# Gate choice, bias spreading and experts in one program, in all four mixture layers of an eight-layer graph model

## The chip, the cores and the metric

One core of one Trainium2 chip runs the whole model in one launch. The metric is the device time of the launch in microseconds, the median of three runs. The compute engines are TensorE (PE; its weight loads are shown as PEld), VectorE (DVE), ScalarE (ACT) and GpSimd (POOL); SyncE (SP) issues DMAs. They run their own instruction streams and meet through semaphores. All numbers here are float32.

## The reference

x is [32, 256, 128]: 8192 tokens of 128 features. Eight layers follow one another, each added to x after a row normalisation. Four of them are mixtures of experts, and only these change:

```python
x = x + _L0_ffn_ref(_layernorm(x), ...)   # 8 experts, gelu, weights = 2 largest of softmax(logits)
x = x + _L1_ffn_ref(_layernorm(x), ...)   # 4 experts, gelu, scores from a graph attention, softmax over top 2
x = x + _L2_ffn_ref(_layernorm(x), ...)   # 6 experts of three products, relu, softmax of the softmax's top 2
x = x + _L3_ffn_ref(_layernorm(x), ...)   # 8 experts, relu, softmax over top 2
# each of them, for a token: sum over experts e of  gate[e] * (act(x @ W1[e] + b1[e]) @ W2[e] + b2[e])
```

gate[e] is zero for all but two experts. The kernel splits the last bias off: it adds the sum of gate[e] * b2[e] with one small product for all experts.

## The kernel before

**Tiles.** x stays on chip as `top_x`, 64 tiles of 128 tokens. The transposed, normalised x of a layer (`xnT`) is also on chip. Four tiles make a group of 512 columns; there are NG = 16 groups.

**Stages.** Each layer is a row of stages, each an `nc.Block` with one program for each engine; a stage starts when all engines have ended the one before. In the mixture layers, written l0f, l1f, l2f and l3f in the names of tiles, the last two are the gates stage (`gates`, L379) and the experts stage (`slotted_experts`, L559, in l0f and l3f; `experts`, L476, in l1f; `experts3`, L977, in l2f).

**The gates stage.** PE makes one product (L403) with every expert's bias for every lane, and ACT spreads it into `biases` with 16 activations (L424). DVE meanwhile picks the two largest scores (`top2`, L360 to L367), hands one tile to ACT for an exponential (L428 or L430; in l2f there is a second one, L433), and works out the gates; its last instruction (L469) writes `top_gate`. PE then turns the gates (L407), ACT copies them (L435, `gT`), and PE and DVE go through the 16 groups: a product `gT` times `biases` (L415) into one of two PSUM buffers `pb`, and the add to x (L472). PE may run two groups ahead of DVE.

**The experts stage.** For each group and expert there is a step. Its up part is two products of 512 columns into `pu` (L495 in l1f, L627 in l0f and l3f); ACT turns each into `h` (L523, L768) with gelu or relu; its down part is eight products of 128 columns into `py` (L503, L635); DVE adds `py` times the gate to x with four instructions (L536, L855). PE issues the up part of the next expert before the down part of this one. A down part waits for its own two `h` tiles and for DVE's add of two steps before; an up part waits until ACT has freed one of four `pu` buffers; `h` waits for the down part of two steps before. In l2f a step is one product (L998), ACT, one product (L1004), ACT, and four products of 128 columns (L1011), three steps deep. Groups are hardware loops (`Fori`) on PE and ACT, and written out on DVE.

**The slots of l0f and l3f.** Only half of the tiles go through all experts. The tokens of the other 32 tiles are sorted by expert into slots: two ranking products on PE (L620, L621) into `tp`, a chain on DVE (L798 to L815) that ends with `slots_ready`, 64 indirect DMAs by POOL that scatter the rows (L714, one pair for each add of DVE), and a slot stage after the first FIRST = 4 groups, that is after 32 steps. In l0f DVE also does counting work for a later layer beside the steps (`fill`, up to 1.7 us a step; L1630, L1636), and in both `owners()` hands out small pieces of work one by one.

Of the kernel before, what the change touches and what calls it, by code (L numbers as in the profile page):

```python
# [7 lines left out]
P = 128  # L8
# [4 lines left out]
GRP = 4  # L13
# [365 lines left out]
def gates(nc, g, tag, E, kind, b2, logits=None, score_bias=None, scores=None, choice=None):  # L379

    with Scope(nc, tag) as s:
        s.rev8 = g.rev8
        lg = s.sb("lg", [P, T, E])
        sel1, sel2, w1, w2 = choices(s, E) if choice is None else choice
        tmp = s.sb("tmp", [P, T, E])
        m1 = s.sb("m1", [P, T])
        m2 = s.sb("m2", [P, T])
        rr = s.sb("rr", [P, T])  # L390
        e2 = s.sb("e2", [P, T])
        su = s.sb("su", [P, T])
        gT = s.sb("gT", [P, T // BLOCK, P])
        biases = s.sb("biases", [P, BLOCK, D])
        pr = s.ps("pr", [P, COLS])
        pw = s.ps("pw", [P, COLS])
        pb = s.ps("pb", [P, 2, COLS])
        (dve_step, exp_in, exp_out, gate_ready, spread_mm, spread_done, gt_mm, gt_copied, bias_mm, bias_added) = s.sems(
            "dve_step", "exp_in", "exp_out", "gate_ready", "spread_mm", "spread_done", "gt_mm", "gt_copied", "bias_mm", "bias_added")
        with nc.Block() as block:  # L400
            @block.tensor
            def _(pe):
                nc.tensor.matmul(pw[:, 0:D], g.expert_lanes[0:E, :, :].rearrange("e t k -> e (t k)"), b2,  # L403
                                 start=True, stop=True).then_inc(spread_mm, 1)
                pe.wait_ge(gate_ready, 1)
                for q in range(T // BLOCK):
                    last = nc.tensor.transpose(pr[:, bass.ts(q, P)], g.gate[:, bass.ts(q, BLOCK), :].rearrange("p t e -> p (t e)"),  # L407
                                               g.ident[:, :])
                last.then_inc(gt_mm, 1)
                pe.wait_ge(spread_done, BLOCK)  # L410
                pe.wait_ge(gt_copied, 1)
                for m in range(NG):
                    if m >= 2:
                        pe.wait_ge(bias_added, m - 1)
# [61 lines left out]
def experts(nc, g, tag, xnT, E, W1, b1, W2, CH, func):  # L476

    with Scope(nc, tag) as s:
# [5 lines left out]
        with nc.Block() as block:  # L485
            @block.tensor
            def _(pe):
# [3791 lines left out]
```

## Time and profile before

| | us |
|---|---|
| runs | 5020.86, 5023.57, 5030.29 |
| median | 5023.57 |
| profiled execution | 5024.53 |
| its span in the trace | 5022.8 |

Busy shares over the span: PE 69%, DVE 67%, ACT 34%, POOL 20%. The model is a row of stages with different limits, so these shares say little on a change within four of them; the views of those stages say more.
### The profile page before, as it was taken

How to read it: one execution, taken by the hardware profiler on the slowest of the kernel's cores; microseconds unless marked ns; L12 is line 12 of the kernel's file. 1: busy time of each engine (PE TensorE's matmuls, PEld its weight loads, DVE VectorE, ACT ScalarE, POOL GpSimd, SP SyncE). 2: the span in 40 equal slices, each digit the busy share in tenths (PEclk: the TensorE clock that was granted, in tenths of full speed). 3: DMA queues.
4: the chain of work that ended last, by engine and by line, in shares of the span. 5: the costliest groups of instructions: out<-in, count | busy, mean ns of one | idle time of the engine just before them, and what ended most of it. 6: DMA issues, size and time to landing. Idle time of an engine off the chain costs nothing. (4 is left out here: it accounts for less than half of the span.)

```text
span 5022.8 us, 67345 instructions
## 1 busy us (share of the span) xinstructions
PE 3450.1 (69%) x17032; PEld 2647.6 (53%) x17034; DVE 3350.8 (67%) x17506; ACT 1694.9 (34%) x4351; POOL 1009.0 (20%) x1111
## 2 busy tenths in 40 slices
PE   7888854552330022779966588889899789786997
PEld 6888844551110021557744477757745346575675
DVE  7998998779998998477756566643334544425444
ACT  2222233334342221034435122244365345432343
POOL 0000000325542001024410477600001000000414
PEclk9999999999755555989978555589999899887999
DMA  3000000000000000112211311000000000000022
GB/s 110 18 1 1 1 1 1 22 1 1 1 1 1 1 1 0 35 46 66 56 35 52 33 9 9 8 0 0 3 1 0 10 1 0 4 1 18 30 85 63
DMA packets 140877, 91.16 MB, mean 18 GB/s; under 512 B 61356, under 2 KB 128902, under 8 KB 139526
## 3 DMA queue, kind: packets, MB, share of 16 engines
q1 hardware_dynamic: 111622, 67.10, 5.2%
q0 software_dynamic: 28928, 20.50, 2.2%
q8 instruction: 107, 1.75, 0.2%
q14 instruction: 220, 1.80, 0.1%
HBM read 51.72 MB, written 35.82 MB: 17 GB/s over the span
## 5 line engine op out<-in xcount | busy, mean ns | idle before, releaser
L1889 POOL DMA_INDIRECT e_sorted<-top_e_pair,top_e_pos x320 | 311.3, 973 | 1514.7 <-DVE top_e_pos L1859 872.8
L2226 POOL DMA_INDIRECT l1f_gas_rs<-l1f_ga_table_s,l1f_ga_slots x320 | 324.6, 1014 | 113.6 <-issue 97.3
L3006 PE MATMUL l0g_tri_late<-l0g_tri_ya,l0g_tri_Z 128*128 128x2 f32 x762 | 202.8, 359 | 176.0 <-DVE l0g_tri_Z L2888 174.3
L3006 PEld LDWEIGHTS l0g_tri_late<-l0g_tri_ya,l0g_tri_Z 128*128 128x128 f32 x762 | 182.2, 318 | 199.9 <-DVE l0g_tri_Z L2888 197.1
L3313 PE MATMUL l0g_val_sums<-l0g_val_sg,l0g_val_fold 128*128 128x156 bf16 (+1 forms) x381 | 102.4, 283 | 263.6 <-DVE l0g_val_sg L3382 212.2
L3592 PE MATMUL l0g_vec_tp<-top_ident,top_x 128*128 128x128 f32 x64 | 16.8, 416 | 318.4 <-ACT top_x L3624 318.4
L2350 PE MATMUL l1f_gas_acc<-l1f_gas_ohh,l1f_gas_ohl 128*128 128x64 bf16 x1280 | 178.5, 302 | 82.8 <-DVE l1f_gas_ohh L2253 82.8
L2981 PE MATMUL l0g_tri_prod<-l0g_tri_Z,l0g_t_As 128*128 128x1 f32 x508 | 148.8, 362 | 125.6 <-DVE l0g_tri_Z L2921 108.2
L3313 PEld LDWEIGHTS l0g_val_sums<-l0g_val_sg,l0g_val_fold 128*128 128x128 bf16 x381 | 39.5, 104 | 327.1 <-DVE l0g_val_sg L3382 273.5
L2986 PE MATMUL l0g_tri_dots<-l0g_tri_Z 128*128 128x7 f32 (+31 forms) x762 | 210.4, 397 | 0.6 <-DVE l0g_tri_Z L2926 0.3
L2981 PEld LDWEIGHTS l0g_tri_prod<-l0g_tri_Z,l0g_t_As 128*128 128x128 f32 x508 | 127.3, 311 | 150.2 <-DVE l0g_tri_Z L2921 129.4
L2350 PEld LDWEIGHTS l1f_gas_acc<-l1f_gas_ohh,l1f_gas_ohl 128*128 128x128 bf16 x1280 | 145.5, 144 | 100.0 <-DVE l1f_gas_ohh L2253 100.0
L1044 DVE SCALAR_TENSOR_TENSOR top_x<-l2f_e_py,top_gate,top_x 128x128 f32<-128x128 f32 x384 | 108.1, 344 | 134.5 <-PE l2f_e_py L1011 132.9
L1482 ACT ACTIVATE l2g_ls_gt<-l2g_ls_acc,lstm_bias 128x512 f32<-128x512 f32 (+1 forms) x252 | 141.0, 637 | 157.4 <-PE l2g_ls_acc L1466 116.8
L1464 PE MATMUL l2g_ls_acc<-l2g_ls_xs,lstm_WihT 128*128 128x512 f32 (+1 forms) x408 | 179.8, 539 | 18.5 <-ACT l2g_ls_gt L1482 18.5
L2986 PEld LDWEIGHTS l0g_tri_dots<-l0g_tri_Z 128*128 128x128 f32 x762 | 191.7, 332 | 1.1 <-DVE l0g_tri_Z L2926 0.9
L3592 PEld LDWEIGHTS l0g_vec_tp<-top_ident,top_x 128*128 128x128 f32 x64 | 12.6, 220 | 319.8 <-issue 259.9
L1447 POOL COPY l2g_ls_xs<-l2g_hT 128x512 f32<-128x512 f32 (+1 forms) x56 | 43.7, 786 | 651.2 <-DVE l2g_hT L1514 487.6
L536 DVE SCALAR_TENSOR_TENSOR top_x<-l1f_e_py,top_gate,top_x 128x128 f32<-128x128 f32 x256 | 72.0, 343 | 138.5 <-PE l1f_e_py L503 138.5
L2991 PE MATMUL l0g_tri_own<-l0g_tri_Z,l0g_tri_eye 128*128 128x1 f32 (+7 forms) x508 | 154.5, 395 | 0.0
L855 DVE SCALAR_TENSOR_TENSOR top_x<-l3f_e_py,top_gate,top_x 128x128 f32<-128x128 f32 x256 | 72.0, 344 | 122.6 <-PE l3f_e_py L635 122.6
L2370 PEld LDWEIGHTS l1f_gas_acc<-l1f_gas_msg,l1f_gas_hot 128*128 128x128 f32 x640 | 142.9, 331 | 0.0
(1074 smaller groups left out, 10548.4 us busy)
## 6 DMA issues: line engine op xcount, KB each, us to landing
e_sorted<-top_e_pair,top_e_pos POOLq DMA_INDIRECT x320, 2.1
l1f_gas_rs<-l1f_ga_table_s,l1f_ga_slots POOLq DMA_INDIRECT x320, 2.4
slot_rows<-l0g_t_nought SPq DMA_DIRECT2D x1, 4608.0 KB, 18.8
l0f_e_xs<-slot_rows SPq DMA_DIRECT2D x18, 256.0 KB, 5.4
slot_outs<-l0f_e_ys SPq DMA_DIRECT2D x18, 256.0 KB, 4.6
l3f_e_xs<-slot_rows SPq DMA_DIRECT2D x18, 256.0 KB, 3.1
slot_outs<-l3f_e_ys SPq DMA_DIRECT2D x18, 256.0 KB, 2.4
out_dram<-top_x SPq DMA_DIRECT2D x2, 2048.0 KB, 12.2
```

The costliest lines, as they stand in the source:

```text
L1044: last = nc.vector.scalar_tensor_tensor(g.x[:, t, :], py[:, e % 2, k, :], g.gate[:, t, e:e + 1], g.x[:, t, :], ALU.mult, ALU.add)
L1464: last = nc.tensor.matmul(out, WihT[:, p - 1, bass.ts(k, P)], x_t, start=True, stop=(st == 0))
L1482: last = nc.scalar.activation(wide(gt[:, n % 2, k, :], n), wide(acc[:, n % 2, k, :], n), f, bias=bias[:, p - 1, k:k + 1])
L1889: nc.gpsimd.indirect_dma_start(out=g.sorted, out_offset=bass.IndirectOffsetOnAxis(ap=g.pos[:, j:j + 1].bitcast(U32), axis=0), in_=g.pair[: ...
L2226: nc.gpsimd.indirect_dma_start(out=rs[:, b, c, :], out_offset=None, in_=table_s, in_offset=bass.IndirectOffsetOnAxis(ap=slots[:, t, c, 0:1 ...
L2350: last = nc.tensor.matmul(hist, ohl[:, n % 2, :, c], ohh[:, n % 2, :, c], start=False, stop=False)
L2370: last = nc.tensor.matmul(acc[:, t // PER, at:at + ROWS], hot[:, t % HB, c, :], msg[:, t % 2, c, :], start=(c == 0 and t < 2 * PER), stop= ...
L2981: nc.tensor.matmul(prod[hs[0]][:, 0:1], As[:, hs[0], bass.ts(hs[0], P)], Z[:, b, hs[0], 0:1], start=True, stop=(hs[0] == 1))
L2986: last = nc.tensor.matmul(dots[:, 0:1 + 2 * J], Z[:, b, h, 0:1].to_broadcast([P, P]), Z[:, b, h, 0:1 + 2 * J], start=(h == hs[0]), stop=(h ...
L2991: last = nc.tensor.matmul(own[:, 0:1 + 2 * J], eye[:, h1, r:r + 1].to_broadcast([P, P]), Z[:, b, h1, 0:1 + 2 * J], start=True, stop=True)
L3006: last = nc.tensor.matmul(late[:, 0:2], Z[:, b, h, 1 + 2 * J:2 + 2 * J].to_broadcast([P, P]), ya[:, h, r, :], start=(h == hs[0]), stop=(h ...
L3313: nc.tensor.matmul(sums[:, 0:wd], fold[:, :] if k < M - 1 else fold_low[:, :], sg[:, k, 0:wd], start=(k == 0), stop=False)
```

## The change

The gates stage is gone as a stage of its own. Its parts become methods of a class `Gates`, and the three experts stages call them:

- PE issues the bias product of all lanes first, then the first expert steps. Ahead of the down part of step 2 (counted over all groups) it does the gates' turning, and ahead of the down parts of steps 2 to 17 one bias product each. For that the first groups are written out on PE. In l0f and l3f the ranking products and a wait for `slots_ready` stand at step 2 as well.
- ACT spreads the biases, does `h` of experts 0 to 2, then the exponentials and the copy of the turned gates, then `h` of expert 3 and on.
- DVE does the whole choice first, then its adds; behind add n (1 to 16) it waits for that add's end, adds bias group n - 1, and in the end waits for that too.
- In PSUM, the bias products alternate between two buffers: one half of `tp` and the router's `logits` in l0f and l3f, a new one and `logits` in l2f, two new ones in l1f.

The core of the diff:

```diff
-def gates(nc, g, tag, E, kind, b2, logits=None, score_bias=None, scores=None, choice=None):
+class Gates:
+    def turn_gates(self, pe):
+        pe.wait_ge(self.gate_ready, 1)
...
+        last.then_inc(self.gt_mm, 1)
+        pe.wait_ge(self.spread_done, BLOCK)
+        pe.wait_ge(self.gt_copied, 1)
+
+    def bias_product(self, pe, m):
+        if m >= 2:
+            pe.wait_ge(self.bias_added, m - 1)
+        self.nc.tensor.matmul(self.pb[m % 2], self.gT[:, m * GRP // BLOCK, :],
+                              self.biases[:, bass.ts(m % (BLOCK // GRP), GRP), :].rearrange("p t d -> p (t d)"),
+                              start=True, stop=True).then_inc(self.bias_mm, 1)
+
+    def beside(self, pe, n):
+        if n == 2:
+            self.turn_gates(pe)
+        if 2 <= n < NG + 2:
+            self.bias_product(pe, n - 2)
...
+    def add_bias(self, dve, m):
+        dve.wait_ge(self.bias_mm, m + 1)
+        nc.vector.tensor_tensor(g.x[:, bass.ts(m, GRP), :], g.x[:, bass.ts(m, GRP), :],
+                                self.pb[m % 2].rearrange("p (k d) -> p k d", k=GRP), ALU.add).then_inc(self.bias_added, 1)
...
@@ experts (l1f), PE @@
-                with pe.Fori(0, NG) as i:
+                def group(i, first=None):
                     up(i, 0)
                     for e in range(E):
                         if e + 1 < E:
                             up(i, e + 1)
+                        if first is not None:
+                            gates.beside(pe, first + e)
                         down(i, e)
+                for i in range(EARLY):
+                    group(i, i * E)
+                with pe.Fori(EARLY, NG) as i:
+                    group(i)
@@ ACT @@
+                gates.spread_biases(act)
...
+                for e in range(E):
+                    if e == 3:
+                        gates.exponentials(act)
+                    hidden(0, e)
@@ DVE @@
+                gates.choose(dve)
                 for n in range(NG * E):
...
                     last.then_inc(added, 1)
+                    if 1 <= n <= NG:
+                        dve.wait_ge(added, n + 3)
+                        gates.add_bias(dve, n - 1)
+                        dve.wait_ge(gates.bias_added, n)
...
@@ slotted_experts (l0f, l3f), PE @@
+                        if first is not None:
+                            if first + e == 2:
+                                ranks()
+                                gates.turn_gates(pe)
+                                pe.wait_ge(slots_ready, 1)
+                            if 2 <= first + e < NG + 2:
+                                gates.bias_product(pe, first + e - 2)
                         down(i, e)
@@ DVE @@
                 for n in range(FIRST * E):
                     add(n)
+                    if 1 <= n <= NG:
+                        dve.wait_ge(added, n + 3)
+                        gates.add_bias(dve, n - 1)
                     next(work, None)
+                    if 1 <= n <= NG:
+                        dve.wait_ge(gates.bias_added, n)
                     fill(1.7)
...
@@ experts3 (l2f), PE and ACT @@
                     for step in range(E + 2):
+                        if first is not None and step >= 2:
+                            gates.beside(pe, first + step - 2)
...
+                hidden(0, range(3))
+                gates.exponentials(act)
+                hidden(0, range(3, E + 1))
```

PE at l0f, before: the gates stage up to the start of the experts stage. `pw` is the product of all biases, `pr` the turned gates, `pb` the 16 bias products, `tp` the ranking; the loop over groups starts with L627.

```order
L403 MATMUL l0f_g_pw<-l0f_l0f_b,top_expert_lanes 128x128
L407 MATMUL l0f_g_pr<-top_ident,top_gate 128x128 x4
L415 MATMUL l0f_g_pb<-l0f_g_biases,l0f_g_gT 128x512 x16
L400 UNCONDITIONAL_BRANCH
L615 UNCONDITIONAL_BRANCH
L620 MATMUL l0f_e_tp<-l0f_e_both,top_ones 128x256
L621 MATMUL l0f_e_tp<-l0f_e_both,l0f_e_lower 128x256
```

PE at the same place now. `pu` are up parts, `py` down parts; `tp` and `logits` are the two buffers of the bias products.

```order
L398 MATMUL l0f_e_tp<-l0f_l0f_b,top_expert_lanes 128x128
L672 MATMUL l0f_e_pu<-l0f_xnT,l0f_l0f_W 128x512 x4
L680 MATMUL l0f_e_py<-l0f_l0f_W,l0f_e_h 128x128 x8
L672 MATMUL l0f_e_pu<-l0f_xnT,l0f_l0f_W 128x512 x2
L680 MATMUL l0f_e_py<-l0f_l0f_W,l0f_e_h 128x128 x8
L672 MATMUL l0f_e_pu<-l0f_xnT,l0f_l0f_W 128x512 x2
L665 MATMUL l0f_e_tp<-l0f_e_both,top_ones 128x256
L666 MATMUL l0f_e_tp<-l0f_e_both,l0f_e_lower 128x256
L405 MATMUL l0f_r_logits<-top_ident,top_gate 128x128 x4
L414 MATMUL l0f_e_tp<-l0f_e_g_biases,l0f_e_g_gT 128x512
L680 MATMUL l0f_e_py<-l0f_l0f_W,l0f_e_h 128x128 x8
```

Four up parts and two down parts now stand ahead of the turning, and each bias product ahead of a down part.

ACT at l0f, before: from the last rows of the spreading to the first `h`.

```order
L424 ACTIVATE l0f_g_biases<-l0f_g_pw,top_zero,top_tile_lanes 128x128 x16
L428 ACT_TABLE_LOAD
L428 ACTIVATE l0f_g_tmp<-l0f_g_tmp 128x512
L435 ACTIVATE l0f_g_gT<-l0f_g_pr 128x512
L400 UNCONDITIONAL_BRANCH
```

ACT now: six `h` tiles of experts 0 to 2 and a second table load stand between the spreading and the exponential.

```order
L428 ACTIVATE l0f_e_g_biases<-l0f_e_tp,top_zero,top_tile_lanes 128x128 x16
L823 ACT_TABLE_LOAD
L823 ACTIVATE l0f_e_h<-l0f_e_pu,l0f_l0f_b 128x512 x6
L436 ACT_TABLE_LOAD
L436 ACTIVATE l0f_e_g_tmp<-l0f_e_g_tmp 128x512
L443 ACTIVATE l0f_e_g_gT<-l0f_r_logits 128x512
L823 ACT_TABLE_LOAD
```

In l1f it reads the same, and in l2f and l3f, whose function is relu, without the first and the third table load.

## Rows read from the trace of the kernel before

**Rows 1.** Intervals, two for each layer: stretch, us, then busy us of each engine (count), PE clock, DMA.

```profile
2181.45:2219.58 38.13, 20.60 (x42) 7.92 (x43) 25.48 (x38) 9.49 (x20) 0.80 (x4) 0.73 0.03 7
2219.58:2335.00 115.42, 112.27 (x641) 81.47 (x639) 103.20 (x397) 47.84 (x67) 62.07 (x64) 1.00 0.16 56
3282.31:3314.15 31.84, 19.70 (x38) 7.16 (x39) 18.11 (x34) 8.07 (x20) 0.00 (x0) 0.72 0.00 1
3314.15:3538.00 223.85, 223.85 (x1276) 162.64 (x1277) 86.57 (x369) 108.27 (x144) 0.00 (x0) 1.00 0.00 0
4065.96:4100.70 34.74, 18.46 (x38) 6.51 (x39) 23.52 (x41) 8.36 (x20) 0.00 (x0) 0.75 0.00 0
4100.70:4357.00 256.30, 256.26 (x1152) 158.69 (x1152) 122.85 (x500) 131.99 (x192) 0.00 (x0) 1.00 0.00 0
4638.49:4673.81 35.32, 20.57 (x43) 7.92 (x43) 23.14 (x36) 7.83 (x19) 0.80 (x4) 0.76 0.00 0
4673.81:4786.00 112.19, 112.19 (x641) 81.47 (x639) 47.08 (x155) 43.98 (x64) 62.35 (x64) 1.00 0.11 38
```

**Rows 2.** Timeline of l0f, gates stage: start, duration, engine, instruction, [idle before, releaser].

```profile
2181.45 0.46 PE L403 MATMUL l0f_g_pw<-l0f_l0f_b,top_expert_lanes 8*128 8x128 f32 x2 [0.32 <-PEq L216]
2181.95 5.70 ACT L424 ACTIVATE l0f_g_biases<-l0f_g_pw,top_zero,top_tile_lanes 128x128 f32<-128x128 f32 x16 [1.20 <-PE l0f_g_pw L403]
2187.66 1.28 ACT L428 ACT_TABLE_LOAD   x1
2190.86 0.63 ACT L428 ACTIVATE l0f_g_tmp<-l0f_g_tmp 128x512 f32<-128x512 f32 x1 [1.92 <-DVE l0f_g_tmp L448]
2195.99 0.69 DVE L469 TENSOR_TENSOR top_gate<-l0f_g_tmp,l0f_g_lg 128x512 f32<-128x512 f32 x1
2198.63 18.07 PE L415 MATMUL l0f_g_pb<-l0f_g_biases,l0f_g_gT 128*128 128x512 f32 x32 [0.78 <-ACT l0f_g_gT L435]
```

**Rows 3.** Timeline of l0f, first steps of the experts stage.

```profile
2219.58 3.60 PE L627 MATMUL l0f_e_pu<-l0f_xnT,l0f_l0f_W 128*128 x8
2219.86 0.42 DVE L798 COPY l0f_e_total<-l0f_e_tp 128x256 f32<-128x256 f32 x1 [1.43 <-PE l0f_e_tp L621]
...
2223.02 1.95 PE L635 MATMUL l0f_e_py<-l0f_l0f_W,l0f_e_h 128*128 128x128 f32 x16
...
2225.11 0.20 DVE L815 CAST l0f_e_slot<-l0f_e_slot_f 128x64 int32<-128x64 f32 x1
...
2226.52 1.95 PE L635 MATMUL l0f_e_py<-l0f_l0f_W,l0f_e_h 128*128 128x128 f32 x16
```

**Rows 4.** Intervals of one us in which the PE clock changed (l0f twice, l2f).

```profile
2184.00:2185.00 1.00, 0.00 (x0) 0.00 (x0) 0.97 (x2) 1.00 (x4) 0.00 (x0) 0.56 0.00 0
2204.00:2205.00 1.00, 1.00 (x3) 0.35 (x2) 0.69 (x1) 0.00 (x0) 0.00 (x0) 0.70 0.00 0
4085.00:4086.00 1.00, 1.00 (x4) 0.42 (x2) 0.29 (x1) 0.00 (x0) 0.00 (x0) 0.83 0.00 0
```

**Rows 5.** Timeline of the gates stages of l1f, l2f and l3f.

```profile
3288.83 1.28 ACT L430 ACT_TABLE_LOAD   x1
3290.12 0.26 ACT L430 ACTIVATE l1f_g_e<-l1f_g_e 128x64 f32<-128x64 f32 x1
...
3292.41 0.43 DVE L469 TENSOR_TENSOR top_gate<-l1f_g_tmp,l1f_g_lg 128x256 f32<-128x256 f32 x1
...
4073.64 0.52 ACT L428 ACTIVATE l2f_g_tmp<-l2f_g_tmp 128x384 f32<-128x384 f32 x1 [0.18 <-DVE l2f_g_tmp L448]
...
4077.06 0.26 ACT L433 ACTIVATE l2f_g_e<-l2f_g_e 128x64 f32<-128x64 f32 x1 [2.90 <-DVE l2f_g_e L458]
...
4079.61 0.56 DVE L469 TENSOR_TENSOR top_gate<-l2f_g_tmp,l2f_g_lg 128x384 f32<-128x384 f32 x1
...
4647.44 0.26 ACT L430 ACTIVATE l3f_g_e<-l3f_g_e 128x64 f32<-128x64 f32 x1 [1.46 <-DVE l3f_g_e L461]
...
4650.25 0.69 DVE L469 TENSOR_TENSOR top_gate<-l3f_g_tmp,l3f_g_lg 128x512 f32<-128x512 f32 x1
```

More of the change, by code:

```diff
@@ L479, in experts @@
+def experts(nc, g, tag, xnT, E, W1, b1, W2, CH, func, kind, b2, scores):
     with Scope(nc, tag) as s:
@@ L482, in experts @@
         py = s.ps("py", [P, 2, GRP, P])
+        pb = [s.ps(f"pb{k}", [P, COLS])[:, :] for k in range(2)]
+        gates = Gates(nc, g, s, E, kind, b2, pb, scores=scores)
+        EARLY = -(-(NG + 2) // E)
         up_ready, h_ready, y_ready, added = s.sems("up_ready", "h_ready", "y_ready", "added")
@@ L673, in slot_down @@
                     last.then_inc(y_slot, 1)
-                with pe.Fori(0, FIRST) as i:
-                    all_experts(i)
+                for i in range(FIRST):
+                    all_experts(i, i * E)
+                pe.wait_ge(gates.bias_added, NG)
                 pe.wait_ge(owners_ready, 1)
@@ L760, in _, with all_experts @@
                 act.sem_inc(h_ready, 4)
-                def all_experts(i):
+                gates.spread_biases(act)
+                def all_experts(i, first=False):
                     for e in range(E):
+                        if first and e == 3:
+                            gates.exponentials(act)
                         act.wait_ge(y_ready, i * E + e + 1)
@@ L992, in _, with group @@
                 pe.sem_inc(mm3, 2)
-                with pe.Fori(0, NG) as i:
+                gates.spread_products(pe)
+                def group(i, first=None):
                     for step in range(E + 2):
+                        if first is not None and step >= 2:
+                            gates.beside(pe, first + step - 2)
                         if step < E:
@@ L1013, in _ @@
                             last.then_inc(mm3, 1)
+                for i in range(EARLY):
+                    group(i, i * E)
+                with pe.Fori(EARLY, NG) as i:
+                    group(i)
             @block.scalar
@@ L1018, in _, with hidden @@
                 act.sem_inc(act2, 2)
-                with act.Fori(0, NG) as i:
-                    for step in range(E + 1):
+                gates.spread_biases(act)
+                def hidden(i, steps):
+                    for step in steps:
                         if step < E:
@@ L1032, in _ @@
                                                  bias=b2[:, e:e + 1]).then_inc(act2, 1)
+                hidden(0, range(3))
+                gates.exponentials(act)
+                hidden(0, range(3, E + 1))
+                with act.Fori(1, NG) as i:
+                    hidden(i, range(E + 1))
             @block.vector
@@ L4147, in attention_routed_layer @@
                    w[n + "ln_gamma"], w[n + "ln_beta"], scores, g.lstm)
[L4148 to L4149 removed]
+        experts(nc, g, "l1f_e", xnT, 4, w1, b1, w2, 2, ACT.Gelu, "top", b2[:, :], scores)
 def skip_lstm_layer(nc, g, w):
```

240 lines of the change are left out of this document (122 added, 118 removed).

## Prediction, before the changed kernel was run

> **What bounds the kernel now.** I read the intervals of the four mixture layers first [rows 1]. Each layer has two: from the first product of the gates stage to the first up part of the experts, and the experts up to their end or, in l0f and l3f, to the slot stage. In the second kind TensorE is busy for 112.27 of 115.42 us, all of 223.85, all of 256.30 and all of 112.19, at the full clock: the steps are paced by PE. DVE has 103.20 of 115.42 us in l0f, but 39 to 48% elsewhere. In the first kind PE works for 18 to 21 of 31.84 to 38.13 us, and the experts wait for the whole of it. These four add up to 140 us, and the change can only move what is in them; it puts their products into steps that PE bounds. Whatever it brings is work of PE that gets done while DVE chooses, and the end of the stage change.
>
> The timeline of l0f [rows 2] shows the gates stage. ACT spreads for 5.70 us and then has time: its exponential waits 1.92 us for DVE. DVE finishes the gates with 2195.99 + 0.69 = 2196.68, PE starts the bias products 1.95 us later at 2198.63, and these take 18.07 us. The first up part comes at 2219.58 [rows 3], 2.9 us after the last product (18.07 us from 2198.63). Two down parts start 3.50 us apart, which is the step. Four products of an up part pair take 3.60 us with the tail, so one takes 0.86, an up part 1.72 and a down part 1.78.
>
> **The sum of each layer.** I count from the first product of the gates stage. L is the length of the first interval [rows 1], t the time at which the first bias product can start in the changed kernel, D the expert work that PE has done by then, c what a lowered clock costs after t. The 16 bias products each add 0.86 us to a step, 13.8 in all, because PE has no idle time there to take them. The layer changes by t - D + 13.8 + c - L.
>
> **D.** Ahead of the turned gates stand four up parts and two down parts: 4 x 1.72 + 2 x 1.78 = 10.4 us in l0f, l1f and l3f. In l2f it is four first, three second and two third products, 9 x 0.87 = 7.8.
>
> **t in l0f.** This is where I expect most of the gain to be lost, since ACT now does three experts' `h` ahead of the exponential. Spreading ends at 6.2 (2187.65 - 2181.45), the table load for gelu takes 1.28, two `h` tiles of 0.69 each end at 9.0. PE has done two up parts by 4.0 and waits 5 us for them. The clock fell about 2.2 us after PE had stopped in l0f (0.56 is the mean of the interval from 2184.00, PE had ended with 2181.91), and it came back 6.0 us into the bias products of l0f (0.70 from 2204.00, start 2198.63) and 3.2 us into those of l2f (0.83 from 4085.00, start 4079.61 + 0.56 + 1.95 = 4082.12) [rows 2, 4, 5]. So I take the first down part at half clock, 3.5 us, to 12.6; the up part of expert 2 follows, partly at half, and its two `h` tiles end at 16.0. Then comes the load of the exponential's table, 1.28, and the exponential, 0.63: 17.9, where before it ended at 10.0. From its end to the gates' end DVE needs 2196.68 - 2191.49 = 5.2 [rows 2]: 23.1. PE must also wait for `slots_ready`, whose chain is behind the gates on DVE: 2219.86 to 2225.31 is 5.45 us [rows 3]. t = 28.7. By then PE has idled again and is slow; between 3.2 and 6.0 us at half clock lose 1.6 to 3.0, c = 2.3. The layer changes by 28.7 - 10.4 + 13.8 + 2.3 - 38.1 = -3.7.
>
> **l3f** is relu, so the first table load falls away: `h` of expert 0 at 7.7, the down part at half clock to 11.3, `h` of expert 2 at 15.1, load and exponential at 16.6, DVE 4650.94 - 4647.70 = 3.24 [rows 5], 19.9, slots 25.4, c = 2.3. The change is 25.4 - 10.4 + 13.8 + 2.3 - 35.3 = -4.2.
>
> **l1f** has no slots. Its clock is low at the start, so the first two up parts take to about 7; `h` of expert 0 ends at 9.2, and whether the clock falls in the 2 us between I can't tell. If it doesn't, `h` of expert 2 ends at 13.7, load and exponential at 15.2, DVE needs 3292.84 - 3290.38 = 2.46 [rows 5], and 1.95 more give t = 19.6; if it does, 21.4. I take 20.1, nearer to the first, with c = 0, as PE idles only for a us or two around the turning: 20.1 - 10.4 + 13.8 - 31.8 = -8.3.
>
> **l2f** waits for the gates in two pieces. `h` of expert 0 is at 6.9, three products at half clock to 12.2, the second `h` of expert 1 at 13.0, load and exponential at 14.9, then 4077.06 - 4074.16 = 2.9 to the second exponential, 0.26, and 4080.17 - 4077.32 = 2.85 to the gates: 20.9 [rows 5], t = 22.8. PE idled for 4 us before, c = 2.3. The change is 22.8 - 7.8 + 13.8 + 2.3 - 34.7 = -3.6.
>
> **DVE.** An add of a bias group took 0.69 us before and takes that again, plus two short waits, 0.8 together. In l1f, l2f and l3f it has room. In l0f its 103.20 us of work lie on 32 steps and the slot chain, some 3.3 a step, and with 0.8 it is 4.1 against a PE step of 3.50 + 0.86 = 4.36. That fits, barely. PE's product m waits for the bias add m - 2, which has two steps of slack. POOL's scatters start 15 us earlier and are released by the same adds as before, and the 115 us of steps still cover them.
>
> **Sum:** -3.7 - 4.2 - 8.3 - 3.6 = -19.8. From the profiled execution's 5024.5 this gives 5004.7; the median of the runs is 1.0 below that execution, so 5003.7.
>
> **Bounds.** If the clock never falls, the same walk gives t = 25.9, 22.6, 19.1 and 19.7 in l0f, l3f, l1f and l2f with c = 0, and changes of -8.8, -9.3, -9.3 and -9.0: -36.4, 4987. If it falls wherever it can and stays low for 6 us each time, the layers give -2.5, -2.9, -6.5 and -2.9: -14.8, 5009.
>
> **A rule on the table loads.** A load and its exponential take no more than 1.28 + 0.01 + 0.26 us in l1f, and the load began with the end of the spreading [rows 5]: a switch of tables costs 1.3 us here. The Trainium skill (ScalarE: Activation LUTs, What ACT_TABLE_LOAD costs) says that every switch takes a drain of about 1.38 us besides, 2.66 in all. By it, an estimate, the six loads that now stand ahead of the exponentials would cost 6 x 1.38 = 8.3 us more and the time would be 5012. The row speaks against it, and the sum goes by the row.
>
> **The rivals.**
>
> *The clock stays up* (4987). PE idles 5 us or more in l0f and l2f, and the same idle lowered the clock in rows 4, so this is unlikely as a whole; 0.12.
>
> *DVE sets the pace in l0f.* The 4.1 us a step is a mean, and steps with row statistics have 0.85 more. If DVE needs 5 us where PE needs 4.36, 16 steps lose 0.65 each, 10 us, and the time is 5014. For it speaks that PE already loses 3 us in l0f and nowhere else [rows 1]; against it, that PE may run two steps ahead. 0.13.
>
> *The bias adds get between PE's steps, and it ends slower.* Every one of the 64 bias products waits for an add of DVE, which in turn waits for its own add and for a product. Before, this alternation cost 18.07/16 = 1.13 us a product instead of 0.86 [rows 2], with nothing else on DVE. If PE had to wait the whole 0.69 us in each of the 64 steps, that is +44 us: 5048. It decides from 19.8/64 = 0.31 us of PE waiting per product on. Against it: DVE is idle for more than half of the steps in three layers. 0.04.
>
> *The products hide* in gaps of PE, and the gain is larger by up to 55 us. With PE busy for all of three intervals there are no gaps; 0.01. That the change does not do what it says is excluded by the order of instructions.
>
> **How the numbers follow.** The forecast, between 4998 and 5009 for its unknown clock, has 0.70. What a measurement of this kernel can tell from no change is about 0.2%, 10 us: faster means below 5013.5. Forecast and high clock lie there, and a part of the DVE rival: 0.87. The rest of that rival and a forecast that is off by twice its spread are within 0.2%: 0.09. Slower: 0.04. The range that holds 8 in 10 takes in the high clock at one end and most of the DVE rival at the other: 4988 to 5015.
>
> **What would show it.** In the trace of the changed kernel the exponential of l0f ends 17 to 19 us after the first product instead of 10, and the gates 23 us after it; the first bias products start at about 28.7, 25.4, 20 and 22.8 us; steps with a bias product are 4.36 us apart and others 3.50; the PE clock is low from the wait for `h` of expert 0 until the first steps after the turning. The prediction is wrong if ACT reaches the exponential before `h` of expert 2, if a step with a product is longer than 4.5 us, or if a stage that the change does not touch moves by more than 3 us.

## The result, and the profile of the changed kernel

The changed kernel takes 5009.4 us (median of 9 runs, 5002.1 to 5016.0), the kernel before 5029.5 us (median of 9, 5020.9 to 5032.0). The ratio is 0.996, with a 95% interval of 0.9952 to 0.9968. The medians differ by 20.1 us; 19.8 had been forecast. The forecast time itself was 5003.7 us, since it started from the earlier median of 5023.6; 5009.4 lies inside the range of 4988 to 5015. The profiled executions differ by only 14.8 us (span 5008.0 against 5022.8), and the rows say why.

The first view is the table of intervals, here with each layer as one stretch, from the first product of the spreading to the last down part ahead of the slots or the next stage. The columns are as in [rows 1]. First the kernel before:

```profile
2181.45:2331.85 150.40, 132.87 (x682) 89.39 (x682) 125.52 (x422) 57.33 (x87) 62.87 (x68) 0.93 0.12 42
3282.31:3538.62 256.31, 244.17 (x1318) 170.23 (x1318) 104.97 (x406) 116.33 (x163) 0.00 (x0) 0.96 0.00 0
4065.96:4356.96 291.00, 274.71 (x1190) 165.21 (x1190) 146.33 (x541) 140.35 (x212) 0.00 (x0) 0.97 0.00 0
4638.49:4786.07 147.58, 132.82 (x682) 89.39 (x682) 70.21 (x191) 51.81 (x83) 63.16 (x68) 0.94 0.09 29
```

The same four stretches of the changed kernel:

```profile
2185.24:2331.28 146.04, 132.84 (x682) 92.41 (x682) 125.58 (x422) 54.35 (x85) 64.24 (x68) 0.95 0.13 44
3283.05:3529.93 246.88, 241.61 (x1318) 170.52 (x1318) 105.63 (x406) 97.94 (x149) 0.00 (x0) 0.99 0.00 0
4059.47:4345.47 286.00, 275.79 (x1190) 167.35 (x1190) 146.49 (x541) 139.91 (x212) 0.00 (x0) 0.98 0.00 0
4628.61:4771.97 143.36, 133.92 (x682) 93.02 (x682) 70.86 (x191) 51.16 (x83) 63.53 (x68) 0.95 0.09 30
```

The layers are 4.4, 9.4, 5.0 and 4.2 us shorter, 23.0 in all. PE's busy time is nearly what it was; what has gone is idle time. In this pair of executions 8.2 us of the 23.0 are lost again in code that the change does not touch: the stretch ahead of l0f is 3.8 us longer, the stretches between the four layers are 1.3, 2.2 and 1.6 us longer, and the one behind l3f is 0.7 us shorter.

The timeline of l0f answers [rows 2]; idle time and releaser stand in brackets.

```profile
2185.24 0.46 PE L398 MATMUL l0f_e_tp<-l0f_l0f_b,top_expert_lanes 8*128 8x128 f32 x2 [0.47 <-PEq L216]
2185.63 3.70 PE L672 MATMUL l0f_e_pu<-l0f_xnT,l0f_l0f_W 128*128 128x512 f32 x8
2185.73 5.71 ACT L428 ACTIVATE l0f_e_g_biases<-l0f_e_tp,top_zero,top_tile_lanes 128x128 f32<-128x128 f32 x16 [1.35 <-PE l0f_e_tp L398]
2191.46 1.28 ACT L823 ACT_TABLE_LOAD   x1
2194.08 3.31 PE L680 MATMUL l0f_e_py<-l0f_l0f_W,l0f_e_h 128*128 128x128 f32 x16 [4.75 <-ACT l0f_e_h L823]
2198.73 1.49 ACT L823 ACTIVATE l0f_e_h<-l0f_e_pu,l0f_l0f_b 128x512 f32<-128x512 f32 x2 [3.55 <-PE l0f_e_pu L672]
2200.24 1.28 ACT L436 ACT_TABLE_LOAD   x1
2201.53 0.63 ACT L436 ACTIVATE l0f_e_g_tmp<-l0f_e_g_tmp 128x512 f32<-128x512 f32 x1
2202.19 0.69 DVE L463 TENSOR_REDUCE l0f_e_g_su<-l0f_e_g_tmp 128x64 f32<-128x512 f32 x1 [7.19 <-ACT l0f_e_g_tmp L436]
2206.66 0.69 DVE L481 TENSOR_TENSOR top_gate<-l0f_e_g_tmp,l0f_e_g_lg 128x512 f32<-128x512 f32 x1
2207.41 0.66 PE L405 MATMUL l0f_r_logits<-top_ident,top_gate 128*128 128x128 f32 x4 [3.55 <-DVE top_gate L481]
2212.97 2.05 PE L414 MATMUL l0f_e_tp<-l0f_e_g_biases,l0f_e_g_gT 128*128 128x512 f32 x2 [4.90 <-DVE l0f_e_slot L872]
2214.80 3.62 PE L680 MATMUL l0f_e_py<-l0f_l0f_W,l0f_e_h 128*128 128x128 f32 x16
2218.22 2.04 PE L672 MATMUL l0f_e_pu<-l0f_xnT,l0f_l0f_W 128*128 128x512 f32 x4
2220.09 1.02 PE L414 MATMUL l0f_r_logits<-l0f_e_g_biases,l0f_e_g_gT 128*128 128x512 f32 x2
2220.95 1.95 PE L680 MATMUL l0f_e_py<-l0f_l0f_W,l0f_e_h 128*128 128x128 f32 x16
```

The chain can be read downwards. ACT spreads, loads a table, and only then gives PE its first `h`: PE has waited 4.75 us. ACT waits 3.55 us in turn for up part 2. The exponential ends at 2202.16, 16.9 us after the start (forecast 17.9, before 10.0); DVE had waited 7.19 us for it. The gates end at 22.1 (forecast 23.1), and the first bias product starts at 27.7 (forecast 28.7), after 4.90 us of waiting for the slots. It takes 2.05 us and the down part behind it 3.62, both at half clock; the next product comes 7.12 us after the first. From 2220.09 on the products are 4.36 us apart, except at the end of each group of 8 steps, where two distances of 2.64 and 6.08 us make the same 8.72 us for two steps (the last expert of a group has no up part behind it, the first has two).

### The profile page after: what moved, and what is told of

It reads as the page before. It is cut to its first block and busy times, and to the rows that moved or that the text cites. A ratio compares the mean times of both kernels' runs of the same rounds, so it can differ in the third digit from the quotient of the medians.

```text
span 5008.0 us, 67053 instructions
## 1 busy us (share of the span) xinstructions
PE 3459.1 (69%) x17034; PEld 2661.4 (53%) x17034; DVE 3353.6 (67%) x17506; ACT 1672.2 (33%) x4335; POOL 1010.1 (20%) x1111
## 3 DMA queue, kind: packets, MB, share of 16 engines
q14 instruction: 221, 1.81, 0.1%
## 5 line engine op out<-in xcount | busy, mean ns | idle before, releaser
L680 PEld LDWEIGHTS l0f_e_py<-l0f_l0f_W,l0f_e_h 128*128 128x128 f32 x1024 | 126.2, 196 | 33.4 <-issue 27.4
L680 PEld LDWEIGHTS l3f_e_py<-l3f_l3f_W,l3f_e_h 128*128 128x128 f32 x1024 | 126.7, 196 | 32.2 <-issue 28.0
```

What stands on the lines that cost most here:

```text
L680: last = nc.tensor.matmul(py[:, e % 2, k, :], h[:, e % 2, c, bass.ts(k, P)], W2[:, e, c, :], start=(c == 0), stop=(c == CH - 1))
```

## The experiments

The lengths of the four layers below are taken as in the two tables above. "t" is the time from a layer's start to its first bias product. A "-" stands where a layer has no such product beside its steps, or where its gates stage stands by itself. In only_l1f and l1f_alone the other three layers are those of the kernel before. The sums and lengths are of one profiled execution each, the ratios of 4 to 12 runs.

```
kernel         l0f len/t       l1f len/t       l2f len/t       l3f len/t       sum     ratio to before [95%]
before         150.40 / -      256.31 / -      291.00 / -      147.58 / -      845.3   1
after          146.04 / 27.7   246.88 / 19.1   286.00 / 22.8   143.36 / 25.2   822.3   0.996  [0.9952, 0.9968]
exp_second     142.52 / 24.3   246.00 / 18.3   278.75 / 17.2   141.15 / 24.1   808.4   0.9929 [0.9915, 0.9942]
exp_first      146.25 / 28.3   249.57 / 21.8   282.85 / 21.4   145.44 / 27.0   824.1   0.9953 [0.9939, 0.9966]
warm           141.89 / 26.3   246.92 / 19.2   281.22 / 19.7   138.14 / 22.6   808.2   0.9936 [0.9922, 0.9949]
second_ranks   138.96 / 21.5   246.00 / 18.3   278.60 / 17.1   135.24 / 19.6   798.8   0.9904 [0.9888, 0.9921]
best           137.32 / 21.4   245.98 / 18.3   277.66 / 16.2   135.08 / 19.5   796.0   0.9908 [0.9891, 0.9924]
adds_first     133.93 / 25.4   246.00 / 18.3   277.69 / 16.2   132.47 / 23.9   790.1   0.9895 [0.9880, 0.9909]
h_first        133.91 / 25.4   246.32 / 16.9   277.66 / 16.2   132.46 / 23.9   790.4   0.9907 [0.9894, 0.9921]
no_products    132.72 / -      236.38 / -      272.71 / -      129.92 / -      771.7   one run, 4965.5 us
dve_twice      149.00 / 28.5   250.18 / 20.8   285.99 / 22.8   143.12 / 25.0   828.3   one run, 5010.1 us
only_l1f       150.41 / -      280.86 / -      291.45 / -      147.64 / -      870.4   1.0044 [1.0031, 1.0058]
l1f_alone      150.31 / -      246.85 / 19.1   291.19 / -      147.63 / -      836.0   0.9991 [0.9981, 1.0]
```

Where two kernels have the same code in a layer, its lengths agree within 0.5 us, except in l1f, of which more below. The total is far less steady, so the layers carry the argument and the ratios confirm it.

**Does the order of ACT set t?** The exponential is moved ahead of the `h` of expert 1 (exp_second), in l2f in two pieces.

```
                 for e in range(E):
-                    if e == 3:
+                    if e == 1:
                         gates.exponentials(act)
+                    if e == 3:
+                        gates.copy_turned(act)
                     hidden(0, e)
```

> The exponential (with its table load) stands right behind the h of expert 0 on ACT in all four layers, in l2f the second exponential behind h of the next step; the copy of the turned gates stays where it was. Theory (the prediction's term t: the bias products start late because the exponential stands behind three experts' h): the exponential of l0f ends near 10.8 us after the stage's start instead of 16.9, the gates near 16 instead of 22.8, the first bias product near 21.5 instead of 27.7; l3f -6, l2f -6, l1f -2.5 us (there PE's own two up and two down parts end only at 16.8). Together about -20 us against the changed kernel: ratio to the kernel before 0.992. Rival (the h tiles behind the exponential come as much later as the gates come earlier, so PE's work D is late instead): within 4 us of the changed kernel, ratio 0.996.

The layers are 3.5, 0.9, 7.3 and 2.2 us shorter than in the changed kernel, 13.9 in all, where 20 were expected; the ratio is 0.9929. ACT's order did delay the gates: in l0f `top_gate` is ready at 2198.76, 15.9 us after the start, as expected (the changed kernel has it at 22.1, not at 22.8 as the expectation says). Then DVE waits, as the timeline of exp_second shows, first l0f and then l3f:

```profile
2198.07 0.69 DVE L486 TENSOR_TENSOR top_gate<-l0f_e_g_tmp,l0f_e_g_lg 128x512 f32<-128x512 f32 x1
2198.70 1.88 PE L679 MATMUL l0f_e_pu<-l0f_xnT,l0f_l0f_W 128*128 128x512 f32 x4
2200.86 0.59 PE L673 MATMUL l0f_e_tp<-l0f_e_both,l0f_e_lower 128*128 128x256 f32 x2
2201.59 0.42 DVE L864 COPY l0f_e_total<-l0f_e_tp 128x256 f32<-128x256 f32 x1 [2.83 <-PE l0f_e_tp L673]
...
4634.35 0.42 DVE L864 COPY l3f_e_total<-l3f_e_tp 128x256 f32<-128x256 f32 x1 [5.72 <-PE l3f_e_tp L673]
```

The rank products stand on PE behind the fourth up part. As long as the gates were late nobody waited for them; now the slot chain does, 2.83 and 5.72 us. The gain was turned into a new wait. In l1f, where there are no slots, only 0.9 of the expected 2.5 us came: PE's first down part still starts at 9.1 us, and its second one now waits 0.38 us for `h`, since ACT has to load the table of gelu again behind the exponential (1.28 us).

**And if the exponential goes first of all?**

```
                 for e in range(E):
-                    if e == 3:
+                    if e == 0:
                         gates.exponentials(act)
```

> The exponentials stand ahead of every h on ACT, right behind the spreading. Theory: the gates come at about 15 us in l0f, but the h of expert 0 waits for the exponential (DVE hands it over 9.4 us after the start), so PE has its two down parts done only near 22 us, and the clock falls in the longer wait: first bias product near 22 in l0f and 21 in l3f, 17.8 in l1f, 16.5 in l2f with PE's pieces late; 12 to 20 us better than the changed kernel, ratio 0.992 to 0.994. Rival (the order of ACT does not matter): ratio 0.996.

The layers are together 1.8 us longer than in the changed kernel, and the ratio is 0.9953, the interval of which overlaps that of the changed kernel. The expectation of 12 to 20 us was wrong. The `h` of expert 0 now waits for the exponential, PE stands still for 8.96 us in l0f instead of 4.75, and t is later by 0.6 us in l0f, 2.7 in l1f and 1.8 in l3f. In l0f the late parts of PE hold up the rank products too, for which DVE waits 7.12 us. In l1f the wait is only 0.5 us longer than in the changed kernel (3.67 against 3.19), but the first down part now runs at half clock, 3.79 us instead of 2.05, so part of the loss there is the clock's. Only l2f, without slots and with two exponentials, gains: 3.2 us. Earlier gates are worth little if PE's own parts are late by as much: t is the later of the two chains, not the gates' alone.

**What does the fallen clock cost?** Products that nobody reads fill PE's waits.

```
+    def warm(self, pe, out, w, x, n):
+        for _ in range(n):
+            self.nc.tensor.matmul(out, w, x, start=True, stop=True)
...
                         if first is not None:
+                            if first + e == 0:
+                                gates.warm(pe, py[:, 1, :, :].rearrange("p k d -> p (k d)"), W1[:, 0, 0:P], xnT[:, 0:COLS], 3)
```

> Extra products whose result nobody reads fill PE's three long waits (before the first down part, before the turning where that wait is long, and for the slots), 3 to 5 at each place, so that the granted clock has no idle stretch in which to fall. The computation is the same. Theory (term c and the half-speed down parts): in l0f the first down part takes 1.9 instead of 3.3 us and those after it less too, the first down part behind the slots 1.9 instead of 3.6: about -4 us in l0f, -5 in l3f, -3.5 in l2f, 0 in l1f, together -12 us against the changed kernel, ratio 0.9935. Rival (the lowered clock costs nothing, as ACT and DVE set the pace there until the first bias product): only the 1.8 us per fall behind t in three layers, -5 us, ratio 0.995. Or the extra products run over into needed ones: slower than the changed kernel.

The layers are 4.2, 0, 4.8 and 5.2 us shorter, 14.1 in all, against 12 expected. In l0f the first down part takes 2.05 us instead of 3.31, and behind the slots the granted clock is up too. So the clock did not only cost what stood behind t: t is 1.4 us earlier in l0f, 3.1 in l2f and 2.6 in l3f, half of the 14.1, because `h` of expert 2 no longer waits for slow up and down parts. The rival (5 us in all) failed.

**The rank products earlier, and both together.**

```
                 def all_experts(i, first=None):
                     up(i, 0)
                     for e in range(E):
+                        if first == 0 and e == 1:
+                            ranks()
```

> As exp_second, and the two rank products of the slot layers stand on PE behind the first down part instead of behind the fourth up part. Theory (in exp_second DVE had the gates of l0f at 15.9 us after the start but then waited 2.83 us for the rank products, in l3f 5.72 us): the slot chain follows the gates at once, the first bias product of l0f comes at 21.5 instead of 24.3 and that of l3f at 19.8 instead of 24.1 (PE's up parts end at 17.4 there), together -7 us against exp_second: ratio to the kernel before 0.9915. Rival (something else holds the slots, or the two products push PE's down part back by as much): within 2 us of exp_second, 0.993.

l0f is 3.6 us and l3f 5.9 us shorter than in exp_second, 9.6 in all with the other layers (7 expected); t is 21.5 and 19.6, as expected to 0.2 us. The ratio is 0.9904 (0.9915 expected). This names the wait that had eaten the gain.

> As second_ranks, with extra products that nobody reads in PE's wait ahead of the first down part (5, in l1f and l3f 3) and 3 in the wait for the slots. Theory (the three causes found so far, ACT's order, the place of the rank products and the fallen clock, add up): stage lengths of 138 us in l0f (changed kernel 146.0), 246 in l1f (246.9), 276 in l2f (286.0) and 134 in l3f (143.4), together -28 us against the changed kernel: ratio to the kernel before 0.990. Rival (the gains overlap, as the clock matters only where PE is late): no better than second_ranks, 0.9915.

The layers are 26.2 us shorter than in the changed kernel, near the 28 expected, but only 2.8 us shorter than in second_ranks. By themselves the three steps had brought 13.9, 9.6 and 14.1 us, 37.6 together, so the gains do overlap, as the rival had it. The ratio of 0.9908 can't be told from 0.9904, and does not decide between the two. The clock is granted in full through the slot layers, as the intervals of best show for l0f and l3f:

```profile
2186.58:2323.90 137.32, 135.81 (x698) 91.77 (x698) 125.66 (x422) 54.09 (x85) 64.14 (x68) 1.00 0.14 47
4603.85:4738.93 135.08, 133.58 (x694) 91.39 (x694) 70.89 (x191) 51.13 (x83) 63.12 (x68) 1.00 0.10 32
```

But t is now set by DVE (choice, then the slot chain), and a faster PE only waits longer. In l3f the extra products even ran 1.2 us past the slots (4622.15 to 4623.37).

**The last wait.** In best PE has the turned gates of l0f at 2204.9 and the slots at 2207.96, 3.0 us later; in l3f the distance is 1.4 us. The first bias product needs the buffer in which the rank products lie, and the first down part behind it needs an add of DVE that stands behind the slot chain.

```
+                add(0)
+                add(1)
                 dve.wait_ge(made, 2)
                 dve.wait_ge(ranked, 1)
...
-                            if 2 <= first + e < NG + 2:
-                                gates.bias_product(pe, first + e - 2)
+                            if first + e == 4:
+                                pe.wait_ge(slots_ready, 1)
+                            if 4 <= first + e < NG + 4:
+                                gates.bias_product(pe, first + e - 4)
```

> As best, but in l0f and l3f DVE adds the results of experts 0 and 1 ahead of the slot chain, the bias products and their adds stand two steps later (beside steps 4 to 19), and no extra products fill the wait for the slots. Theory (in best, PE has the turned gates of l0f at 17.7 us after the start and waits until 21.4 for the slots, as the first bias product needs the buffer of the rank products; l3f 16.1 and 19.5): two down parts and two up parts get done in that wait, l0f -4 us and l3f -3.5 against best (137.3 and 135.1): 133.5 and 131.5; ratio to the kernel before 0.989. Rival (the slots come two adds, 2.3 us, later, and PE waits for them all the same two steps on): less than 1.5 us in each layer, ratio 0.9905.

l0f is 3.4 us and l3f 2.6 us shorter than in best (4 and 3.5 expected). PE goes from the turning to the end of the layer with hardly a wait; the timeline of adds_first in l0f:

```profile
2203.63 0.60 PE L409 MATMUL l0f_r_logits<-top_ident,top_gate 128*128 128x128 f32 x4
2204.97 2.02 PE L696 MATMUL l0f_e_py<-l0f_l0f_W,l0f_e_h 128*128 128x128 f32 x16 [0.73 <-issue]
2206.83 1.88 PE L688 MATMUL l0f_e_pu<-l0f_xnT,l0f_l0f_W 128*128 128x512 f32 x4
2208.55 1.95 PE L696 MATMUL l0f_e_py<-l0f_l0f_W,l0f_e_h 128*128 128x128 f32 x16
2210.15 0.19 DVE L909 CAST l0f_e_slot<-l0f_e_slot_f 128x64 int32<-128x64 f32 x1
2212.05 1.02 PE L418 MATMUL l0f_e_tp<-l0f_e_g_biases,l0f_e_g_gT 128*128 128x512 f32 x2
```

The slots are ready 1.7 us ahead of the product that needs them. The ratio is 0.9895, by the medians 51 us below the kernel before, and its layers are 32.2 us shorter than those of the changed kernel. It is the fastest of these kernels by its layers (no_products, which leaves out work, aside); by the ratio alone it can't be told from second_ranks.

**Spreading behind the first `h` in l1f.**

```
                     if e == 1:
                         gates.exponentials(act)
+                    if e == 2:
+                        gates.spread_biases(act)
                     if e == 3:
                         gates.copy_turned(act)
```

> As adds_first, and in l1f ACT does the h of expert 0, the exponential and the h of expert 1 ahead of the spreading; no extra products in l1f. Theory (5.7 us of spreading stand ahead of the first h, and PE's own parts set t there at 18.3): PE has no long wait ahead of its first down part, the first bias product comes at 15 to 16 us and l1f takes 243.5 us instead of 246.0. Rival (the copy of the turned gates now waits behind the spreading, 14 us, and the h of expert 2 behind both): l1f 246 or longer.

The rival held. t is 1.3 us earlier, but l1f is 0.3 us longer. The timeline of h_first:

```profile
3287.86 0.66 PE L409 MATMUL l1f_e_pb<-top_ident,top_gate 128*128 128x128 f32 x4 [1.81 <-ACT l1f_e_g_biases L432]
3289.59 1.75 PE L418 MATMUL l1f_e_pb<-l1f_e_g_biases,l1f_e_g_gT 128*128 128x512 f32 x2 [1.08 <-ACT l1f_e_g_gT L452]
3291.13 3.00 PE L531 MATMUL l1f_e_py<-l1f_l1f_W,l1f_e_h 128*128 128x128 f32 x16
```

PE waits 1.81 and 1.08 us, with the turning between, its clock falls just after the first bias product has begun (0.95 in the interval from 3289, 0.50 in the next), and this product and the down part behind it take 1.75 and 3.00 us instead of 1.10 and 1.95.

**Are the products on PE's path?**

> The changed kernel without its 64 bias products and their adds: the experts' second biases are left out of the result. The turning and the waits for the gates and slots stay. Theory (every product lies on PE's path at 0.86 us): each layer is 13.8 us shorter than in the changed kernel: 132.2, 233.1, 272.2 and 129.5 us, together -55 us, the time 4954. Rival (the products hide in PE's gaps, or DVE paces l0f): less than 10 us shorter in some layer; the l0f rival in particular: l0f shorter by its DVE time only, the others by 13.8. The other rival (the adds get between PE's steps, over 1.1 us a product): more than 18 us shorter per layer.

l0f, l2f and l3f are 13.32, 13.29 and 13.44 us shorter than in the changed kernel, 0.83 to 0.84 us for each of 16 products (0.86 forecast). l1f is only 10.5 shorter, since its clock fell here and not in the changed kernel: the first down part takes 2.58 us behind 3.29 us of waiting, against 2.05 behind 3.19. The same happened in dve_twice, whose l1f has the code of the changed kernel and took 250.18 us; in both the clock fell a second time behind the turning. In dve_twice t is 1.7 us later than in the changed kernel, and the first bias product takes 2.05 us instead of 1.10. Between no_products and dve_twice the difference is 13.8. The first down part and, where there is one, the first bias product of the changed kernel, no_products and dve_twice, in this order:

```profile
3292.18 2.05 PE L522 MATMUL l1f_e_py<-l1f_l1f_W,l1f_e_h 128*128 128x128 f32 x16 [3.19 <-ACT l1f_e_h L550]
...
3302.19 1.10 PE L414 MATMUL l1f_e_pb<-l1f_e_g_biases,l1f_e_g_gT 128*128 128x512 f32 x2 [0.78 <-ACT l1f_e_g_gT L443]
```

```profile
3283.84 2.58 PE L520 MATMUL l1f_e_py<-l1f_l1f_W,l1f_e_h 128*128 128x128 f32 x16 [3.29 <-ACT l1f_e_h L548]
```

```profile
3289.31 2.56 PE L525 MATMUL l1f_e_py<-l1f_l1f_W,l1f_e_h 128*128 128x128 f32 x16 [3.27 <-ACT l1f_e_h L553]
...
3301.00 2.05 PE L414 MATMUL l1f_e_pb<-l1f_e_g_biases,l1f_e_g_gT 128*128 128x512 f32 x2 [0.78 <-ACT l1f_e_g_gT L443]
```

**Does DVE pace l0f?**

```
         dve.wait_ge(self.bias_mm, m + 1)
+        if self.E == 8:
+            spare = self.tmp[:, :, :].rearrange("p t e -> p (t e)").rearrange("p (k d) -> p k d", k=GRP)
+            nc.vector.tensor_tensor(spare, g.x[:, bass.ts(m, GRP), :], self.pb[m % 2].rearrange("p (k d) -> p k d", k=GRP), ALU.add)
```

> In l0f and l3f every bias add has a second add of the same size ahead of it, into a buffer that nobody reads: 0.72 us more on DVE in each of 16 steps, 11.5 us in all. Theory (DVE has 5.5 us of room in l0f's product steps, 66.55 busy of 72.03, and 33 us in l3f's): l0f is 6 us longer, l3f 0. Rival (DVE paces l0f already): l0f 11.5 us longer. Rival (products wait for their adds): both layers longer.

l0f is 3.0 us longer, of which 0.8 had come before the first bias product already; l3f is 0.2 shorter. So 11.5 us more on DVE cost some 2 us in l0f (2.2). The timeline of dve_twice shows the only two waits of PE for DVE from the first bias product to the end of the layer:

```profile
2253.11 2.02 PE L683 MATMUL l0f_e_py<-l0f_l0f_W,l0f_e_h 128*128 128x128 f32 x16 [0.30 <-DVE top_x L915]
2270.29 2.02 PE L683 MATMUL l0f_e_py<-l0f_l0f_W,l0f_e_h 128*128 128x128 f32 x16 [1.02 <-DVE top_x L915]
```

The two waits make 1.3 of the 2.2 us. I had expected 6, because I set DVE's idle time in the 16 product steps (5.5 us) against the added 11.5. But DVE's work need not be done within these steps: it is busy for 71.14 of 71.99 us there, 66.55 of 72.03 in the changed kernel, and catches up in the 14 steps behind (43.4 of 48.5 us busy), while PE may run two steps ahead.

**One layer alone.** only_l1f is told with its mistake: the separate gates stage of l1f had been left in beside the merged program, so l1f's gates were chosen and its biases added twice.

> Only l1f has gates and experts in one program, the other three layers are as before. Theory (each layer has its own share, and nothing else changes): l1f's own stretch is 9.4 us shorter (forecast 8.3), the time 8 to 10 us below the kernel before, ratio 0.998; the stages that are not touched differ by single falls of the clock only. Rival (the 8 us by which untouched stages were longer in the profile of the changed kernel belong to the change): ratio 0.999 or more, and the stages ahead of l0f longer by 3 us again.

It took 22 us more than the kernel before, and l1f was 280.86 us. The separate stage (31.8) and the merged program (246.9 or 250.2, by its clock) make 279 to 282, so even this agrees. Without the stage:

> The kernel before, with gates and experts in one program in l1f alone and without the separate gates stage there. In the run only_l1f that stage had been left in, so that l1f chose its gates and added its biases twice. Theory (each layer has its own share): l1f 246.9 us, or 250.2 where the clock falls in the wait ahead of the first down part, against 256.3 before; the other three layers as before (150.4, 291.0, 147.6); ratio 0.9985. Rival (untouched stages lose what l1f gains): ratio 0.9995 or more.

l1f takes 246.85 us, and the other layers have their old lengths within 0.2 us. The ratio of 0.9991 (0.9981 to 1.0) holds the expected 0.9985 as well as the rival's 0.9995, so 9.5 us is what this measurement can hardly show in the total. In the profiled execution of this kernel the untouched stretches were 4 us shorter than before, so the rival (they lose what the layer gains) finds nothing here. Its other sign, a longer stretch ahead of l0f, does not go with the change either: against the kernel before this stretch is 6.1 us longer in only_l1f, 0.8 in l1f_alone, and 0.3 us shorter in dve_twice, which has the whole change.

## Why the prediction was right, and where its steps were off

**Which wait goes and what replaces it.** This part held. PE's idle stretch for the gates became two or three shorter waits, for the `h` of expert 0, for the gates and for the slots. "ACT now does three experts' `h` ahead of the exponential" was the main loss: exp_second gave back 13.9 us, and second_ranks another 9.6 once the rank products were out of the way.

**The sum.** The layers were forecast at -3.7, -8.3, -3.6 and -4.2 and came at -4.4, -9.4, -5.0 and -4.2. The medians agree to 0.3 us partly by luck: in the profiled pair the layers gained 3.2 us more than the sum, and the rest of the program gave 8.2 us back, which had no term in the sum.

**t.** Forecast 28.7, 20.1, 22.8 and 25.4; measured 27.7, 19.1, 22.8 and 25.2. In l0f I had the clock down for all of the first down part (to 12.6). It was granted in full until PE had started again. The intervals are of the changed kernel, the last one of l3f:

```profile
2193.00:2194.00 1.00, 0.00 (x0) 0.00 (x0) 0.93 (x3) 1.00 (x3) 0.00 (x0) 1.00 0.00 0
2194.00:2195.00 1.00, 0.92 (x6) 0.93 (x7) 1.00 (x2) 1.00 (x3) 0.00 (x0) 0.81 0.00 0
...
2198.00:2199.00 1.00, 1.00 (x4) 0.49 (x3) 0.00 (x0) 0.27 (x1) 0.00 (x0) 0.98 0.00 0
...
4635.00:4636.00 1.00, 0.00 (x0) 0.00 (x0) 0.93 (x3) 1.00 (x3) 0.00 (x0) 0.58 0.00 0
```

So the fall came some 5 us after PE had stopped (2189.33), not 2.2 as in [rows 4], and the down part took 3.31 us instead of 3.5. In l3f of the same execution it came 2.5 us after PE had stopped (4632.69), and the first down part took 3.78 us, all at half clock. In l1f both branches of the forecast (19.6 with the clock up, 21.4 with it down) were seen: 19.1 and 20.8.

**c.** In l0f the step after the slots took 7.12 us instead of 4.36, so c is 2.8 (2.3 forecast). In l2f it was the most off. With the measured t the formula leaves 0.9 where I had 2.3; the rows show 3.43 us for two products that take 1.72 at the full clock, so the clock cost 1.7. Of the 0.8 us between, no_products places 0.5: the 16 products cost 13.3 us there and not 13.8. The rest stays open.

**The products.** 0.83 to 0.86 us each (l1f against dve_twice), on PE's path in every layer, shown by no_products.

**The rivals.** DVE does not set the pace in l0f: 11.5 us more on DVE cost 2. The 3 us of idle PE in l0f that I had put down for this rival do not lie in the steps: they are the 3.15 us from the end of the last down part (2331.85) to the end of the interval (2335.00), and from 2222 to 2331 us PE is busy throughout. The adds do not get between PE's steps: from the first bias product of each layer on, the changed kernel's PE has no wait of 0.1 us or more. The price of 1.13 us a product before was misread too: in l0f the first four starts are 1.84, 1.71 and 1.71 us apart, with the clock low until 2204.6, and once it is up they come every 0.94 to 0.96 us. Most of the 1.13 was the clock, and the alternation with DVE cost 0.1. The clock did fall, and holding it up was worth 14.1 us, near the 16.6 between the forecast and the clock rival.

**The table loads.** In l1f of the changed kernel the exponential starts 1.30 us after its load, as in [rows 5]:

```profile
3296.69 1.28 ACT L438 ACT_TABLE_LOAD   x1
3297.99 0.26 ACT L438 ACTIVATE l1f_e_g_e<-l1f_e_g_e 128x64 f32<-128x64 f32 x1
```

The Trainium skill (ScalarE: Activation LUTs, What ACT_TABLE_LOAD costs) has 1.38 us of drain besides. The rows here do not have it: in l0f the load starts at 2200.24, 0.02 us behind the `h` tiles of 2198.73 + 1.49, and the exponential 0.01 us behind the load.

**What would have proved it wrong.** Two of my signs did come, and show nothing against the mechanism. The first step with a product is longer than 4.5 us in l0f (7.12), which is c. And I had named an untouched stage that moves by more than 3 us. That was a poor test. The whole stretch ahead of l0f was 3.8 us longer, and 2.8 of them are in three rows, first before, then after:

```profile
2034.41 3.42 PE L3971 MATMUL l0g_ref_p<-l0g_ref_X,l0g_Bm 128*128 128x256 f32 x8 [0.62 <-PEq L1065]
2038.60 1.99 PE L3971 MATMUL l0g_ref_p<-l0g_ref_X 128*128 128x256 f32 x8 [0.78 <-DVE l0g_ref_Y L3993]
2040.43 1.89 PE L3971 MATMUL l0g_ref_p<-l0g_ref_Y,l0g_ref_X 128*128 128x256 f32 x8
```

```profile
2035.03 3.75 PE L4058 MATMUL l0g_ref_p<-l0g_ref_X,l0g_Bm 128*128 128x256 f32 x8 [0.62 <-PEq L1152]
2039.56 3.78 PE L4058 MATMUL l0g_ref_p<-l0g_ref_X 128*128 128x256 f32 x8 [0.79 <-DVE l0g_ref_Y L4080]
2043.14 2.54 PE L4058 MATMUL l0g_ref_p<-l0g_ref_Y,l0g_ref_X 128*128 128x256 f32 x8
```

They are the same products in the same order, at up to twice the time while the clock was low. This is 150 us ahead of the first changed instruction. Over the thirteen profiled executions l0f starts anywhere from 2181.1 to 2187.9 us, and all the untouched stretches together take 4173 to 4192 us, whichever kernel it is. Only one piece seems to go with the change: from l2f to l3f it is 281.5 to 282.1 us in the three kernels whose l2f is as before, and 282.2 to 283.9 in the ten others. In the changed kernel two of the DMA issues at the start of the next stage took 0.68 and 1.43 us instead of 0.42 and 0.43. In each of the ten the longest issue there takes 0.60 to 1.84 us, in the three none takes more than 0.47. Why was not tried.

One more sign was off: the clock was not low from the wait for `h` of expert 0 until the first steps after the turning. In l0f it was up again from 2198.0 to 2208.3, and in l1f it did not fall at all.

## What to carry to other kernels

When work is overlapped with a chain of three engines, follow each engine's queue up to the point where the chain comes back to PE. The gain is set by the later of the chains, and each one that is shortened (here ACT's exponential, then the rank products, then two adds) only shows the next. Look for instructions that nobody waited for before and that somebody will wait for now. Before an average is taken as the price of a wait, look at the clock of the rows under it. Compare stage by stage: here the untouched stretches alone differed by up to 19 us between executions.

## What the runs showed of the hardware

- TensorE's granted clock does not always fall at the same point of the same code. The first down part of l1f ran at the full clock behind waits of 3.14 us (l1f_alone) and 3.19 us (changed kernel), partly at half behind 3.27 us (dve_twice) and 3.29 us (no_products), and all of it at half behind 3.67 us (exp_first). Between the changed kernel and dve_twice, which have the same code there, the layer differs by 3.3 us. Whether the tenth of a us in the wait decides this was not tried.
- The length of a wait alone does not tell. In l1f of h_first the clock fell behind waits of only 1.81 and 1.08 us; in l0f of the changed kernel it stayed up through a wait of 4.75 us until PE had started again; in l3f it fell within a wait of 3.31 us.
- Filling waits with products that nobody reads pays where PE is the later chain: 14.1 us in the changed kernel, 2.8 us once DVE's chain was the later one in the slot layers.
- In the four layers of the changed kernel each of the eight table loads took 1.28 us, with 0.01 to 0.02 us of idle ACT before and behind it.
